# The second routing of an eight-block model: expert 0 computed for every token, seven experts routed

## The chip, the cores and the metric

The kernel runs on one core of one Trainium2 chip, as one launch written out engine by engine: five instruction streams (TensorE, VectorE, ScalarE, GpSimd and SyncE) that are ordered among themselves only by semaphores. The metric is the device time of the launch in microseconds, the median of the runs; lower is better.

## The reference, cut to what matters

Four layers, each an attention block and a feed-forward block, over x of 4 x 512 tokens of 128 values (float32). The change is in the feed-forward block of the third layer, a top-2 mixture of 8 experts with a capacity of 640 rows each (2 x 1.25 x 2048 / 8):

```python
logits = xf @ w_g                                   # xf: the 2048 normed tokens
topv, topi = jax.lax.top_k(logits, 2)
probs = softmax(logits where chosen, -1e9 elsewhere)
rank = cumulative count per expert, all first choices before all second choices
mask = one_hot(topi) * (rank < 640)
wts = sum(mask * probs)
cb[token, topi[:, k], rank_sel[k]] += wts[k]        # for k = 0, 1
exp_batches = einsum('nec,nd->ecd', cb != 0, xf)    # rows sent to the experts
h = gelu(einsum('ecd,edh->ech', exp_batches, c_fc), approximate=False)   # 128 -> 512
exp_out = einsum('ech,ehd->ecd', h, c_proj)                              # 512 -> 128
out = einsum('nec,ecd->nd', cb, exp_out)            # added to x by the caller
```

The next block is the cross attention of the fourth layer, and after it a mixture that computes 8 small experts for all tokens.

## The kernel before, in words

**Layout.** Tokens lie in 16 chunks of 128 (4 sequences t = 0 to 3, 4 chunks each). `xs` holds the normed tokens by rows, with the token's number as a 129th value, and `xT` holds them turned, 128 features by 512 tokens for each t. Eight PSUM banks `ps0` to `ps7` of 128 x 512 float32 serve everything.

**Order.** Each engine walks the same lists of stages, SEQ0 to SEQ3, with `wavefront`: stage s of sequence t runs beside stage s+1 of sequence t-1. Between SEQ2 and SEQ3 stands the second routing, named "m2" (the first, "m0", stands between SEQ0 and SEQ1 and has a capacity of 128 rows, so that nothing about it changes here). The order around the change is written out by hand, and a few semaphores carry it: `idx_ready` (row numbers known), `sent` (16 for each finished send), `g_ld`, `gT_m`, `gT_s` (an expert's rows fetched, turned, copied), `h_mm`, `h_act` (a hidden unit multiplied, activated), `gy_mm`, `gy_sb`, `gy_st` (an expert's result multiplied, copied out, stored).

**The second routing, stage by stage.**
- VectorE picks each token's first expert (L1464 to L1468). TensorE counts with matmuls over one-hot rows (L834, L837), VectorE makes row numbers (`places`, L1473 to L1480). GpSimd then sends, one indirect DMA for a chunk of 128 tokens and a choice (`send`, L1857): 16 for the first choices, 16 for the second. They write rows of 516 bytes to the table `tok2` in DRAM, 8 x 640 rows.
- Beside the first sends TensorE counts the second choices (`count_second`, L897 to L908) into bank 2, VectorE copies `first_n` out of it (L1713), makes the second row numbers, and computes the gate weights (L1715 to L1722). TensorE multiplies out keys and values of the next attention (`prepare("L3")`, L870 and L873), and VectorE copies them out (L1507, L1516).
- When all 32 sends have landed (`sent`), SyncE fetches the rows expert by expert (L543), and TensorE runs nine matmuls whose result is not used (`keep_busy`, L913) before it turns the first expert's rows (L949). GpSimd spreads the keys and values by heads (L1888, L1901).
- For each expert VectorE writes the turned rows as two parts, a rounded high part (L1588) and the remainder (L1589). The hidden layer is `product` (L915 to L919): three matmuls, high x high, high x low, low x high, on 320 tokens, for 4 slices f of 128 hidden units and 2 halves, so 24 matmuls. ScalarE applies Gelu from bank 2 + u % 4 into `hid` (L1229). The output layer is 20 float32 matmuls (L981, in the trace two entries for each, so 40). VectorE copies the result to `ysb` (L1614), and GpSimd stores it by five indirect DMAs to the table `res2` (L1930), 2 x 2048 rows, one half for each choice, which was set to zero at the start of the kernel.
- TensorE's order is hidden(0), then for each expert e: hidden(e+1), turning of group e+3, results(e). With five blocks an expert's result takes banks 6 and 7 both.
- After the last store SyncE reads `res2` back (L550), and VectorE adds both halves, weighted by `wgt`, to x (`fetched`, L1623), which is the first step of SEQ3.

**Memory that is shared.** `qTR` and `qT` lie in the same bytes (the attention's queries; `ysb` too lies there), as do `xTR` and `xT`, `bigR` and `big`. `kr` holds rounded keys of the earlier attentions; the one of the fourth layer uses `kvR`. The high parts of the first-layer weights of m2 lie in `ring_r`, the low parts in `moe_r`; both are made long before, beside the attention of SEQ2 (L1840, L1841).

## Time and profile before

| | us |
|---|---|
| median of 3 runs | 693.19 (693.09 to 694.12) |
| profiled execution | 696.29 |
| its span, first to last instruction | 694.5 |
| TensorE busy in the span | 507.6 (73%) |
| VectorE busy | 346.9 (50%) |
| GpSimd busy | 260.4 (37%) |
| ScalarE busy | 218.7 (31%) |
| mean granted TensorE clock | 0.796 of 2.4 GHz |

The profile is of one execution. Times in its rows are microseconds from the start of the span. "PEld" is TensorE's loading of weights, beside its matmuls. A matmul's duration contains the way through the array, and matmuls overlap: what one costs in a row of them is the distance from start to start. A group of matmuls in the timeline is given by its start, its length and its count. What ended an idle time is told from semaphore events; "remote" (in the chain: "another core or an unknown queue") stands where an event came with no instruction that ended just then. The chain follows the last instruction back to whatever released it.

### The profile page before, as it was taken

What the parts mean: (1) busy time and instruction counts of PE and PEld (TensorE: products, weight loads), DVE (VectorE), ACT (ScalarE), POOL (GpSimd) and SP (SyncE); (2) the same over time, 40 slices, a digit from 0 to 9 for tenths busy, and PEclk for the clock granted to TensorE, in tenths of its full rate; (3) what the DMA queues carried; (4) which work ended last, traced back from release to release, by engine and by line L of the source; (5) the groups of instructions that cost most, each with busy time, mean ns of one, the idle gap of its engine ahead of it and who ended that gap; (6) DMA issues with size and microseconds to landing.
All of it is one profiled execution on the core that took longest, in us unless ns stands there. A gap on an engine that the chain in (4) does not pass through costs nothing.

```text
span 694.5 us, 8672 instructions
## 1 busy us (share of the span) xinstructions
PE 507.6 (73%) x3053; PEld 382.2 (55%) x3053; DVE 346.9 (50%) x1111; ACT 218.7 (31%) x423; POOL 260.4 (37%) x372
## 2 busy tenths in 40 slices
PE   4497793648678865697863049998269957999997
PEld 3342472636555451443763029998035346899997
DVE  4749528641098643159874023331286684333333
ACT  3341542102234520051330005331044334344441
POOL 4650757371345101155337751555475051000000
PEclk9679797557865999589555569999659966899999
DMA  9998600001170006750001122111350000000002
GB/s 288 301 143 171 230 1 0 9 22 37 53 259 0 1 0 176 205 166 0 1 0 51 49 75 69 52 48 37 92 160 1 1 1 0 1 1 1 1 1 60
DMA packets 64107, 48.06 MB, mean 69 GB/s; under 512 B 6441, under 2 KB 55877, under 8 KB 63936
## 3 DMA queue, kind: packets, MB, share of 16 engines
q1 hardware_dynamic: 60560, 41.88, 23.3%
q0 software_dynamic: 3072, 5.06, 2.3%
q10 hardware_dynamic: 432, 0.57, 0.3%
q8 instruction: 24, 0.39, 0.2%
q14 instruction: 19, 0.16, 0.1%
HBM read 35.08 MB, written 13.68 MB: 70 GB/s over the span
## 4 chain that ended last, share of the span: by engine, by line
PE 52%; DVE 20%; POOL 10%; issue 7%; DMA 3%; ACT 3%; another core or an unknown queue 2%; SPq 1%; POOLq 0%; ACTq 0%; DVEq 0%
PE ps L1019 9%; PE ps L981 5%; POOL tok L1857 3%; PE ps L917 3%; DVE rz L1406 3%; PE ps L603 3%; DVE st L1319 3%; PE ps L919 3%; PE ps L918 3%; POOL rstd L1765 3%; PE ps L615 3%; PE ps L714 2%; PE ps L657 2%; PE ps L780 2%
## 5 line engine op out<-in xcount | busy, mean ns | idle before, releaser
L1930 POOL DMA_INDIRECT res<-qT,dest x48 | 47.1, 982 | 68.2 <-DVE qT L1614 57.7
L1640 DVE SCALAR_TENSOR_TENSOR x<-ps,gate,x 128x128 f32<-128x128 f32 x128 | 36.1, 345 | 62.9 <-PE ps L1019 62.9
L1019 PEld LDWEIGHTS ps<-moe_w,big 128*128 128x128 f32 x512 | 63.3, 196 | 3.9 <-issue 1.5
L1019 PE MATMUL ps<-moe_w,big 128*128 128x128 f32 x512 | 63.7, 280 | 0.0
L1244 ACT ACTIVATE big<-ps,col 128x512 f32<-128x512 f32 x64 | 44.0, 688 | 59.2 <-PE ps L919 58.8
L1774 POOL TENSOR_SCALAR negmean<-mv 128x4 f32<-128x4 f32 x44 | 11.3, 257 | 127.8 <-DVE mv L1322 126.7
L1857 POOL DMA_INDIRECT tok<-r,to_slot x48 | 47.3, 986 | 31.5 <-DVE to_slot L1480 17.8
L603 PE MATMUL ps<-con,xn 128*128 128x128 f32 x128 | 31.9, 398 | 35.3 <-DVE xn L1335 20.6
L913 PE MATMUL ps<-tri,ones 128*128 128x512 bf16 x46 | 17.7, 562 | 50.2 <-DMA tok<-r,to_slot 25.1
L1195 ACT ACTIVATE xn<-x,negmean,rstd 128x128 f32<-128x128 f32 x48 | 21.1, 486 | 98.8 <-POOL negmean L1777 98.8
L1229 ACT ACTIVATE big<-ps 128x320 f32<-128x320 f32 x64 | 26.7, 441 | 77.8 <-PE ps L919 77.6
L1765 POOL TENSOR_TENSOR rstd<-rstd,half 128x4 f32<-128x4 f32 (+1 forms) x45 | 47.8, 1062 | 3.7
L603 PEld LDWEIGHTS ps<-con,xn 128*128 128x128 f32 x128 | 21.4, 203 | 48.8 <-DVE xn L1335 48.5
L981 PE MATMUL ps<-moe_w,big 128*128 128x128 f32 x384 | 45.7, 275 | 2.7 <-DVE qT L1614 2.7
L981 PEld LDWEIGHTS ps<-moe_w,big 128*128 128x128 f32 x384 | 44.2, 192 | 3.0 <-issue 2.8
L1406 DVE RECIPROCAL rz<-ps 128x512 f32<-128x512 f32 x12 | 40.1, 3346 | 9.6 <-PE ps L733 9.4
L1614 DVE COPY qT<-ps 128x128 f32<-128x128 f32 (+1 forms) x24 | 9.4, 421 | 65.9 <-PE ps L981 40.7
L913 PEld LDWEIGHTS ps<-tri,ones 128*128 128x128 bf16 x46 | 5.7, 132 | 60.4 <-issue 33.6
L633 PE MATMUL ps<-sq,xT 128*128 128x128 f32 x128 | 20.6, 314 | 15.4 <-DVE xT L1408 15.4
L633 PEld LDWEIGHTS ps<-sq,xT 128*128 128x128 f32 x128 | 18.0, 219 | 23.7 <-DVE xT L1408 22.1
L1319 DVE BATCH_NORM_STATS2 st<-x 128x6 f32<-128x128 f32 x128 | 27.9, 281 | 5.8 <-DMA x<-in_x 4.8
L917 PE MATMUL ps<-qTR,moe_r 128*128 128x512 f32 x64 | 29.0, 453 | 2.0 <-DVE oh L1468 2.0
(283 smaller groups left out, 1153.4 us busy)
## 6 DMA issues: line engine op xcount, KB each, us to landing
ring<-in_ew SPq DMA_DIRECT2D x21, 256.0 KB, 5.3
moe_w<-in_m0w SPq DMA_DIRECT2D x16, 256.0 KB, 6.6
moe_w<-in_m2w SPq DMA_DIRECT2D x16, 256.0 KB, 5.8
big<-res SPq DMA_DIRECT2D x12, 256.0 KB, 4.6
moe_w<-in_ew SPq DMA_DIRECT2D x11, 256.0 KB, 5.5
tok<-zero SPq DMA_DIRECT2D x1, 2580.0 KB, 30.9
big<-tok SPq DMA_DIRECT2D x8, 322.5 KB
ring<-in_ewg SPq DMA_DIRECT2D x9, 256.0 KB, 4.6
```

What stands on the lines that cost most here:

```text
L603: last = nc.tensor.transpose(ps[2 * t][:, cols(c)], from_, ident)
L633: last = mm(ps[2 * t + 1][:, cols(c)], xT[0:width, t, cols(c)], w, start=True, stop=True)
L917: mm(o, high, x_high_, start=True, stop=False)
L981: last = mm(o, hid[:, e % 2, f, cols(b)], moe_w[:, e, 512 + P * f:512 + P * f + P], start=f == 0, stop=f == 3 and bias is None)
L1019: last = mm(ps[7 - i % 2][:, cols(c)], big[:, f, i % B, cols(c)], w[:, e, F + P * f:F + P * f + P], start=f == 0, stop=f == FC - 1)
L1244: A(big[:, f, i % B, :], ps[(i * FC + f) % 6][:, :], fn, bias=V(bias, e * FC + f)).then_inc(h_act, 1)
L1319: i = v.bn_stats(st[:, C * t + c, :], d[:, C * t + c, :])
L1406: link(v.reciprocal(rz[:, :], ps[2 * t + 1][:, :]))
L1640: last = v.scalar_tensor_tensor(out=x[:, C * t + c, :], in0=ps[7 - i % 2][:, cols(c)], scalar=gate[:, C * t + c, e:e + 1], in1=x[:, C * t ...
L1765: g_.tensor_tensor(rstd[0:rows, tt], rstd[0:rows, tt], half[0:rows, 0:width], ALU.pow).then_inc(done, 1)
L1857: g_.indirect_dma_start(out=tok_d[name], out_offset=bass.IndirectOffsetOnAxis(ap=to_slot[:, j:j + 1], axis=0), in_=xs[:, j % (B * C), :], ...
L1930: g_.indirect_dma_start(out=res_d[name], out_offset=bass.IndirectOffsetOnAxis(ap=dest[:, at:at + 1], axis=0), in_=ysb[:, e % 2, cols(b)], ...
```

## The change

Expert 0 is no longer routed. It is computed for all 2048 tokens from `xT`, four units of 512 tokens, and the outcome is added to x with the weight `have`, each token's gate for expert 0 in either choice (0 where it was not chosen or over the capacity). Experts 1 to 7 go the old way. All 32 sends stay, the rows for expert 0 too, but these are no longer fetched. The changed parts:

```diff
+        units0 = {"m0": 0, "whole": 4 * E, "m2": 4 * E + C * B}
+        done0 = {"m0": 0, "whole": E, "m2": E + B}
-        PLACED = {"m0": dict(cap=CAP0, eg=4, ranks=1), "m2": dict(cap=CAP2, eg=1, ranks=2)}
+        PLACED = {"m0": dict(cap=CAP0, eg=4, ranks=1, whole=0), "m2": dict(cap=CAP2, eg=1, ranks=2, whole=1)}
+            a["n"] = E - a["whole"]
+        whole_low = kr[:, :].rearrange("p (a n) -> p a n", a=2)
+        whole_y = xn
 # TensorE, in placed("m2"): after count_second and the wait for the second row numbers, ahead of prepare("L3")
+            def whole_expert(loaded):
+                pe.wait_ge(loaded, 32 * E)
+                pe.wait_ge(split, 8)
+                def hidden(t):
+                    pe.wait_ge(low_ready, t + 1)
+                    for f in range(4):
+                        if t >= 1:
+                            pe.wait_ge(h_act, n["h"] - 3)
+                        product(ps[2 + f][:, :], w1_high["m2"][:, 0, cols(f)], w1_low["m2"][:, 0, cols(f)],
+                                qTR[:, t, :], whole_low[:, t % 2, :])
+                        n["h"] += 1
+                    return n["h"]
+                def results(t, units):
+                    pe.wait_ge(h_act, units)
+                    if t >= 2:
+                        pe.wait_ge(gy_sb, done0["whole"] + t - 1)
+                    for c in range(C):
+                        for f in range(4):
+                            last = mm(ps[6 + t % 2][:, cols(c)], hid[:, t % 2, f, cols(c)], moe_w[:, 0, 512 + P * f:512 + P * f + P],
+                                      start=f == 0, stop=f == 3)
+                    last.then_inc(gy_mm, 1)
+                units = hidden(0)
+                for t in range(B):
+                    nxt = hidden(t + 1) if t + 1 < B else None
+                    results(t, units)
+                    units = nxt
 # ScalarE: whole_high() after SEQ2, whole_expert(Gelu) after the exponentials of the gates
+            def whole_high():
+                for t in range(B):
+                    act.wait_ge(xT_ready, 4 * WHOLE_TURN + t + 1)
+                    A(qTR[:, t, :], xT[:, t, :], ACT.Identity).then_inc(x_high, 1)
+            def whole_expert(fn):
+                for t in range(B):
+                    if t >= 2:
+                        act.wait_ge(gy_mm, done0["whole"] + t - 1)
+                    for f in range(4):
+                        act.wait_ge(h_mm, n["h"] + 1)
+                        A(hid[:, t % 2, f, 0:S], ps[2 + f][:, :], fn).then_inc(h_act, 1)
+                        n["h"] += 1
 # VectorE
+            def whole_low_of(t):
+                dve.wait_ge(x_high, t + 1)
+                if t >= 2:
+                    dve.wait_ge(h_mm, units0["whole"] + C * (t - 1))
+                v.tensor_tensor(whole_low[:, t % 2, :], xT[:, t, :], qTR[:, t, :].bitcast(F32), ALU.subtract).then_inc(low_ready, 1)
+            def whole_out(t):
+                dve.wait_ge(gy_mm, done0["whole"] + t + 1)
+                v.tensor_copy(whole_y[:, chunks(t), :], ps[6 + t % 2][:, :].rearrange("p (c d) -> p c d", c=C)).then_inc(gy_sb, 1)
             places(ps[2][:, E:(nb + 1) * E]..., slice(nb, 2 * nb), CAP2, "base2")
+            whole_low_of(0)
+            whole_low_of(1)
...
             link(v.tensor_reduce(wgt[:, :], gb[:, :, :], AX.X, ALU.add))
+            link(v.tensor_tensor(have[:, 0:nb], gb[:, 0:nb, 0], gb[:, nb:2 * nb, 0], ALU.add))
+            whole_low_of(2)
+            whole_out(0)
+            whole_low_of(3)
+            for t in range(1, B):
+                whole_out(t)
             prepared("L3")
 # VectorE, in evacuate, for each of the seven experts, ahead of the wait for its result
+                    if name == "m2":
+                        for c in range(nb * i_ // a["n"], nb * (i_ + 1) // a["n"]):
+                            i = v.scalar_tensor_tensor(out=x[:, c, :], in0=whole_y[:, c, :], scalar=have[:, c:c + 1], in1=x[:, c, :],
+                                                       op0=ALU.mult, op1=ALU.add)
+                        link(i)
```

Elsewhere the loops over the experts of a routing run over `a["n"]` (8 for m0, 7 for m2), with e = i + `a["whole"]`, and the counts that are waited for begin at `units0` and `done0`. GpSimd issues 35 stores where there were 40, SyncE seven fetches where there were eight.

## Rows read from the trace of the kernel before

**Rows 1.** The page: shares of the chain that ended last, by engine.

```profile
PE 52%; DVE 20%; POOL 10%; issue 7%; DMA 3%; ACT 3%; another core or an unknown queue 2%; SPq 1%; POOLq 0%; ACTq 0%; DVEq 0%
```

**Rows 2.** The chain of 355 to 520 us: start, length, engine and line.

```profile
404.15 2.04 DMA tok<-r,to_slot
...
406.50 4.00 PE ps L913 x9
...
423.56 4.47 PE ps L981 x40
...
494.87 2.08 DMA res<-qT,dest
```

**Rows 3.** Busy time of each engine in stretches; PEclk is the granted clock.

```profile
core 0: us, PE busy (x) PEld busy (x) DVE busy (x) ACT busy (x) POOL busy (x), PEclk, DMA share, GB/s
...
378.80:406.20 27.40, 2.50 (x10) 2.21 (x10) 3.10 (x10) 0.00 (x0) 20.23 (x21) 0.50 0.15 50
406.50:412.20 5.70, 5.06 (x14) 2.22 (x14) 0.60 (x1) 0.00 (x0) 5.05 (x5) 0.50 0.42 116
412.30:482.00 69.70, 64.70 (x507) 63.29 (x507) 22.60 (x61) 28.35 (x65) 29.18 (x30) 1.00 0.19 54
...
428.02:436.98 8.96, 8.96 (x74) 8.96 (x73) 2.98 (x8) 3.44 (x8) 4.89 (x5) 1.00 0.21 58
```

**Rows 4.** Timeline of VectorE: the copying out of experts 0, 1 and 6.

```profile
428.06 0.89 DVE L1614 COPY qT<-ps 128x512 f32<-128x512 f32 x2 [6.89 <-PE ps L981]
...
437.04 0.89 DVE L1614 COPY qT<-ps 128x512 f32<-128x512 f32 x2 [5.89 <-PE ps L981]
...
481.25 0.89 DVE L1614 COPY qT<-ps 128x512 f32<-128x512 f32 x2 [7.87 <-remote]
```

**Rows 5.** Timeline of TensorE in the last mixture, whose hidden product has 512 columns.

```profile
603.78 1.95 PE L1019 MATMUL ps<-moe_w,big 128*128 128x128 f32 x16
...
606.04 0.39 PE L919 MATMUL ps<-qTR,moe_r 128*128 128x512 f32 x1
606.27 0.39 PE L917 MATMUL ps<-qTR,moe_r 128*128 128x512 f32 x1
...
606.97 1.28 PE L1019 MATMUL ps<-moe_w,big 128*128 128x128 f32 x10
```

**Rows 6.** Groups by shape, 592 to 694 us and 406 to 497 us: count, busy, mean ns.

```profile
L1244 ACT ACTIVATE big<-ps,col 128x512 f32<-128x512 f32 x56 | 38.5, 688 | 58.4 <-PE ps L919 58.2
...
L1589 DVE TENSOR_TENSOR xTR<-ps,bigR 128x512 fp32r<-128x512 f32 x8 | 5.5, 692 | 0.3
```

**Rows 7.** Timeline at the end of the counting and at `prepare("L3")`.

```profile
369.57 1.03 PE L906 MATMUL ps<-oh,ones 128*128 128x120 bf16 x15
...
377.39 0.17 DVE L1713 COPY first_n<-ps 128x8 f32<-128x8 f32 x1 [7.63 <-remote]
...
378.63 0.20 DVE L1480 TENSOR_SCALAR to_slot<-slot 128x16 uint32<-128x16 f32 x1
...
379.47 1.92 PE L873 MATMUL ps<-sq,rep 128*128 128x128 f32 x8
...
381.10 0.35 DVE L1507 TENSOR_SCALAR kts<-ps,col 128x128 f32<-128x128 f32 x1
...
392.03 0.69 DVE L1516 TENSOR_TENSOR vr<-ps,row 128x512 f32<-128x512 f32 x1 [10.58 <-remote]
```

**Rows 8.** Timeline of the first routing: VectorE's adds beside GpSimd's sends.

```profile
137.93 4.30 DVE L1651 SCALAR_TENSOR_TENSOR x<-r,drop,x 128x128 f32<-128x128 f32 x16
138.75 0.97 POOL L1857 DMA_INDIRECT tok<-r,to_slot  x1 [0.30 <-issue]
140.03 0.97 POOL L1857 DMA_INDIRECT tok<-r,to_slot  x1 [0.30 <-issue]
```

**Rows 9.** Timeline from the last send to the first expert's transposes and product.

```profile
410.29 1.27 PE L949 MATMUL ps<-con,big 128*128 128x128 f32 x5
...
414.52 0.39 PE L917 MATMUL ps<-bigR,ring_r 128*128 128x320 f32 x1
```

More of the change, by code:

```diff
@@ L105 @@
 BUSY = 14
+WHOLE_TURN = sum(q[0] == "turn" for q in SEQ0 + SEQ1 + SEQ2) - 1
 LAST_TURN = sum(q[0] == "turn" for q in SEQ0 + SEQ1 + SEQ2 + SEQ3) - 1
@@ L541, in placed_traffic @@
                         sp.wait_ge(gT_s, g0 + g - 1)
-                    rows = slice(g * a["gb"] * P, (g + 1) * a["gb"] * P)
+                    rows = slice((a["whole"] + g) * a["gb"] * P, (a["whole"] + g + 1) * a["gb"] * P)
                     sp.dma_start(xg[:, g % 2, 0:a["gb"] * (D + 1)].rearrange("p (b d) -> p b d", d=D + 1),
@@ L951, in turn_group, with hidden @@
                     n["g"] += 1
-                def hidden(e):
-                    g = e // eg
+                def hidden(i):
+                    g, e = i // eg, i + a["whole"]
                     pe.wait_ge(gT_s, g0 + g + 1)
-                    at = (e % eg) * a["cap"]
+                    at = (i % eg) * a["cap"]
                     for f in range(4):
@@ L989, in placed @@
                 units = hidden(0)
-                for e in range(E):
-                    nxt = hidden(e + 1) if e + 1 < E else None
-                    results(e, units)
+                for i in range(a["n"]):
+                    nxt = hidden(i + 1) if i + 1 < a["n"] else None
+                    results(i, units)
                     units = nxt
@@ L1216, in chances @@
                 n["moe"] += 1
+            def whole_high():
[10 more added lines that the diff above has]
+                        n["h"] += 1
             def placed(name, k, fn, bias):
                 a = PLACED[name]
-                for e in range(E):
-                    if e >= 2:
-                        act.wait_ge(gy_mm, k * E + e - 1)
-                    if name == "m2" and e == 1:
+                for i in range(a["n"]):
+                    e = i + a["whole"]
+                    if i >= 2 or name == "m2":
+                        act.wait_ge(gy_mm, done0[name] + i - 1)
+                    if name == "m2" and i == 1:
                         round_keys("L3")
@@ L1593, in group @@
                     number = xg[:, g % 2, 0:gb_ * (D + 1)].rearrange("p (b d) -> p b d", d=D + 1)[:, :, D]
-                    at = (40 if k else 0) + g * gb_
+                    at = (40 if k else 0) + (a["whole"] + g) * gb_
                     if a["ranks"] == 1:
@@ L1604, in evacuate @@
                 group(1)
-                for e in range(E):
-                    g = e // eg
-                    if e % eg == eg - 1 and g + 2 < a["groups"]:
+                for i_ in range(a["n"]):
+                    g = i_ // eg
+                    if i_ % eg == eg - 1 and g + 2 < a["groups"]:
                         group(g + 2)
-                    dve.wait_ge(gy_mm, k * E + e + 1)
-                    if e >= 2 or k:
-                        dve.wait_ge(gy_st[e % 2], stores(name, e // 2))
+                    if name == "m2":
+                        for c in range(nb * i_ // a["n"], nb * (i_ + 1) // a["n"]):
+                            i = v.scalar_tensor_tensor(out=x[:, c, :], in0=whole_y[:, c, :], scalar=have[:, c:c + 1], in1=x[:, c, :],
+                                                       op0=ALU.mult, op1=ALU.add)
+                        link(i)
+                    dve.wait_ge(gy_mm, done0[name] + i_ + 1)
+                    if i_ >= 2 or k:
+                        dve.wait_ge(gy_st[i_ % 2], stores(name, i_ // 2))
                     for j in range(0, nb_, 4):
                         m = min(4, nb_ - j)
-                        i = v.tensor_copy(ysb[:, e % 2, j * P:(j + m) * P], ps[6 + (j // 4 if nb_ > 4 else e % 2)][:, 0:m * P])
+                        i = v.tensor_copy(ysb[:, i_ % 2, j * P:(j + m) * P], ps[6 + (j // 4 if nb_ > 4 else i_ % 2)][:, 0:m * P])
                     i.then_inc(gy_sb, 1)
@@ L1925, in deliver @@
                 a = PLACED[name]
-                for e in range(E):
-                    pool.wait_ge(gy_sb, seen * E + e + 1)
+                for i in range(a["n"]):
+                    pool.wait_ge(gy_sb, done0[name] + i + 1)
                     for b in range(a["nb"]):
-                        at = (40 if seen else 0) + e * a["nb"] + b
+                        at = (40 if seen else 0) + (i + a["whole"]) * a["nb"] + b
                         g_.indirect_dma_start(out=res_d[name], out_offset=bass.IndirectOffsetOnAxis(ap=dest[:, at:at + 1], axis=0),
-                                              in_=ysb[:, e % 2, cols(b)], in_offset=None, bounds_check=a["ranks"] * B * S - 1,
-                                              oob_is_err=False).then_inc(gy_st[e % 2], 16)
+                                              in_=ysb[:, i % 2, cols(b)], in_offset=None, bounds_check=a["ranks"] * B * S - 1,
+                                              oob_is_err=False).then_inc(gy_st[i % 2], 16)
             g_.memset(zero[:, 0:D], 0.0)
```

29 lines of the change are left out of this document (16 added, 13 removed).

## The prediction

> **What bounds the kernel now.** I read the shares of the chain first, then the chain in the second routing, then busy time by stretch, then the timelines. TensorE has 52% of the chain [rows 1]: work that leaves TensorE's path counts, where nothing else is late in its place. In the second routing the chain goes three ways [rows 2]. Up to 404.15 us it is GpSimd's sends, one after another, the last one landed at 406.19. From 406.50 it is TensorE (warm-up matmuls, then the experts). The end is the last store, 494.87 + 2.08. The stretches say why the two halves differ [rows 3]: from 378.80 to 406.20 TensorE is busy for 2.50 of 27.40 us and ScalarE for none, while from 412.30 to 482.00 TensorE has 64.70 of 69.70. The reader is to see an idle engine ahead of a full one. The experts follow each other in TensorE's own time: the copies of experts 0 and 6 start at 428.06 and 481.25 [rows 4], six periods in 53.19, so 8.87 us each. Inside one (428.02 to 436.98) TensorE is busy throughout, VectorE 2.98 us, ScalarE 3.44, GpSimd 4.89 [rows 3]. So one routed expert less is worth 8.87 us, if what replaces it fits ahead of the sends' end.
>
> **What the change removes.** One period of 8.87 us on the path: 24 hidden matmuls, 5 transposes, 40 output entries, 8 activations, VectorE's splitting and copying, five stores, one fetch. The first and the last period keep their neighbours (the last two experts, where GpSimd's stores are the chain, are still 6 and 7), so an inner period goes. The 32 sends stay, and so does their end at 406.19.
>
> **What it adds on TensorE.** For each of four t: 12 products on 512 columns and 16 float32 matmuls, 32 entries. The last mixture shows both forms at full clock [rows 5]: products start 0.23 us apart, and a period from 603.78 to 606.97, 3.19 us, holds 16 output entries and 6 products. With 4.47 us for 40 output entries [rows 2], 0.112 each, 16 take 1.79, and the 6 products the other 1.40, 0.233 each. The whole expert is 48 x 0.233 = 11.2 and 128 x 0.112 = 14.3, together 25.5 us.
>
> **When it can start.** It stands behind the wait for the second row numbers, written at 378.63 + 0.20 = 378.83 [rows 7], and needs the first low part. That subtraction with two SBUF inputs is not in the trace on VectorE; the nearest are the same subtraction with one input in PSUM, 0.69 us [rows 6], and the adds with two SBUF inputs, 4.30 / 16 = 0.27 for 128 columns [rows 8], 1.08 for 512. I take 0.69, since it is the same operation and width: start 379.5. (1.08 would cost 0.4 once.) `qTR` is written by ScalarE before, four copies into an engine that has nothing to do between the last turn and the gates' exponentials; nothing if hidden, 4 x 0.69 = 2.8 if not, still ahead of 378.8.
>
> **The clock.** Up to 406.20 the granted clock is 0.50, 1.2 GHz [rows 3]: TensorE did almost nothing. At the warm-up matmuls it stays at 0.50 for 5.70 us of nearly full work and is 1.00 behind it. I expect the same 5.7 us at the start of the whole expert, which does half the work in it: 2.85 lost. Bounds: 0 and, if the clock never rose, 25.5 more.
>
> **The other engines beside it.** ScalarE: 16 activations of 128x512 by 0.688 [rows 6], 11.0 us of 25.5. Hidden unit t+1 needs bank f back from unit t, four groups of products (2.8 us at full clock) later, so ScalarE's 0.69 for each is in time. VectorE: four low parts and four copies, 8 x 0.69 = 5.5 us; the gate weights wait 1.4 us longer, which nobody does. `have` is one small instruction, 0.3. The 16 adds to x are 4.3 us [rows 8], two or three in each of seven periods, 0.5 to 0.8 on a VectorE that has 2.98 of 8.96: nothing; without that cover 4.3.
>
> **What is late next.** Whole expert: 379.5 + 25.5 + 2.85 = 407.9, so 1.7 behind the sends' landing. `prepare("L3")` now stands behind it: VectorE copies out t = 3 (0.69), then the keys (0.35) and the values (0.69) [rows 6, 7], until 409.7. Queued behind that wait on TensorE are the nine warm-up matmuls; they took 4.00 us [rows 2] at half the clock and should take half of it now: 411.7. Before, the first transposes began at 410.29 [rows 9], so they are 1.4 late; at full clock five take about 0.3 less. Net 1.1 late. GpSimd's spreading of the keys starts about 1.7 later; its user is ScalarE's rounding at 418.8 in the chain, with 7 us to spare.
>
> **The sum.** In the profiled execution: -8.87 + 1.1 = -7.8, 696.29 to 688.5. Not all of it need be paid in other runs. VectorE's copy of `first_n` waits until 377.39, though TensorE's last counting matmul ends at 370.60 [rows 7]. If that signal came in time, the row numbers would be there at 372.0, the whole expert would end at 401.1, and the transposes would wait for nothing new: -8.9, and up to -9.9 if the clock is still up for the warm-up matmuls. The profiled execution is 3.1 us above the median of the runs, so some such wait may be absent from these. I take -8.2, between the two: 693.19 - 8.2 = 685.0 us.
>
> **Rivals.** *Late signals of TensorE during the sends (the other side).* The trace shows two signals of TensorE that arrive long after its matmul ended, both while GpSimd sends: 370.60 to 377.39, 6.8 us, and the values of `prepare` (381.39) to 392.03, 10.6 us [rows 7]. Before, sends hid both. The whole expert has 20 such signals, and ScalarE, then TensorE, wait for them. TensorE can run on for 2.8 us, the next unit's products. One of 10.6 costs 7.8 and eats the gain: 693.2. Two, 10.6 and 6.8, cost 7.8 + 4.0: -7.8 + 11.8, 697.2. It decides from 7.8 us of lost TensorE time on. For it: two long ones among a few in this very stretch. Against it: between 412.30 and 482.00, with stores 29 of 70 us, TensorE is busy for 64.70 and its signals hold up no expert but the last ones [rows 3, 4]. One or two of some 3 to 5 us (part of the gain lost) is more likely: -4, 689.2.
>
> The Trainium skill, SBUF — State Buffer, "Who interferes with whom", says that TensorE and ScalarE never wait on anyone for SBUF, since they have their own ports. By that rule alone TensorE would signal in time and the sum would be -8.9, 684.3; the trace has the two, whatever their cause, so I keep this rival's chances above what the rule would leave.
>
> *The sends are slowed by VectorE.* Eight new instructions of 128x512 run beside sends. If each held GpSimd up for its length, the sends would end 8 x 0.69 = 5.5 later, at 411.7, behind the whole expert: -8.9 + 5.5 = -3.4, 689.8. Against it: in the first routing 16 adds with two SBUF inputs ran from 137.93 for 4.30 us, and sends still started 1.28 apart [rows 8], as in the chain.
>
> *It does not do what it says:* a clock that stays at 0.50 through all of the whole expert. 2 x 25.5 = 51 us from 379.5 end at 430.5, 24.3 behind the sends: -8.9 + 24.3 + 1.7 for `prepare` = +17, 710. Against it: the clock rose at every long run of products seen here [rows 3].
>
> **How the numbers follow.** About 0.2% (1.4 us) is what a measurement of this kernel tells from no change. The forecast (-7 to -10) has 0.58, part of the gain lost 0.17, slower sends 0.04, late signals from 7.8 us on 0.18 (half of it near no change or slightly either way), cold clock 0.03. Faster by over 0.2%: 0.58 + 0.17 + 0.04 = 0.79, less 0.02 for part losses that come near zero, 0.77. Within 0.2%: 0.08. Slower: 0.15. The forecast's own range is 683.3 to 686.5. The range for 8 in 10 goes from 683.0 (-10.2: the better end and a clock that is up) to 693.0, which takes in part losses and slower sends.
>
> **What would show it.** In the profile after: between 379 and 408 TensorE over 90% busy, with PEclk 1.00 from about 385; products on `qTR` and `whole_low` of line `product`; the last copy of `whole_y` near 408 (or 401); the last send unchanged, some 41 us after the first; the warm-up matmuls 0.21 us apart and not 0.43; seven copies of `ysb` 8.87 apart; the last store at 489 instead of 497. Wrong would be: TensorE idle in gaps of several us in the whole expert with ScalarE or VectorE waiting for it (late signals), sends further apart than 1.28, or periods above 8.9 us, which would mean that VectorE's adds are no longer hidden.

## The result, and the profile after

The changed kernel takes 706.82 us (median of 4 runs, 702.80 to 707.63), the kernel before beside it on the same chip 693.14 (691.04 to 694.12): a ratio of 1.0191, 95% interval [1.0152, 1.0229]. It is slower by 13.7 us, where 8.2 us faster was predicted. The time is outside the range of 683 to 693.

The profiled execution of after took 702.8 us, its span 701.0. Everything in it up to the second routing came early: its first send starts at 358.22, that of before at 364.45. In the profiles of this case, of kernels that are alike almost up to that moment, it lies between 357.7 and 364.5, so absolute times of two profiles can't be set against each other. I therefore measure two stretches, each from one event to another of the same profile. **A** is from GpSimd's first send of the second routing to ScalarE's first hidden unit of a routed expert. **B** is from there to the first tile of rows fetched back.

The timeline of VectorE and GpSimd after, at these events and between (start, length, engine, line, what, idle before):

```profile
358.22 1.13 POOL L1938 DMA_INDIRECT tok<-r,to_slot  x1 [8.53 <-DVE to_slot L1538]
...
398.44 0.97 POOL L1938 DMA_INDIRECT tok<-r,to_slot  x1 [0.30 <-issue]
```

```profile
403.98 0.69 DVE L1639 COPY xn<-ps 128x512 f32<-128x512 f32 x1 [20.81 <-PE ps L948]
...
422.36 0.69 DVE L1639 COPY xn<-ps 128x512 f32<-128x512 f32 x1 [2.88 <-PE ps L948]
...
443.46 0.89 DVE L1687 COPY qT<-ps 128x512 f32<-128x512 f32 x2 [5.89 <-issue]
...
487.99 0.89 DVE L1687 COPY qT<-ps 128x512 f32<-128x512 f32 x2 [7.42 <-issue]
...
508.28 2.31 DVE L1696 SCALAR_TENSOR_TENSOR x<-big,wgt,x 128x128 f32<-128x128 f32 x8 [11.34 <-DMA big<-res]
```

The sends are nearly as before, 32 of them, 1.27 us apart but for two, the last one started 40.2 us after the first (before 39.7). The experts are as predicted too: from the first to the sixth copy of results 44.53 us, 8.91 a period (before 8.87, [rows 4]). What is wrong is the whole expert. Its first group of results leaves PSUM at 403.98 and its last at 422.36, where the prediction had the last at 28.4 us behind its first product. ScalarE's timeline shows what happened beside the sends: each row of L1270 is one hidden unit, released by the third product of its group.

```profile
373.56 0.60 ACT L1270 ACTIVATE big<-ps 128x512 f32<-128x512 f32 x1 [10.34 <-PE ps L925]
374.83 0.60 ACT L1270 ACTIVATE big<-ps 128x512 f32<-128x512 f32 x1 [0.68 <-issue]
377.46 0.60 ACT L1270 ACTIVATE big<-ps 128x512 f32<-128x512 f32 x1 [2.03 <-PE ps L925]
382.38 0.60 ACT L1270 ACTIVATE big<-ps 128x512 f32<-128x512 f32 x1 [4.32 <-remote]
386.58 0.60 ACT L1270 ACTIVATE big<-ps 128x512 f32<-128x512 f32 x1 [3.60 <-issue]
390.77 0.60 ACT L1270 ACTIVATE big<-ps 128x512 f32<-128x512 f32 x1 [3.60 <-remote]
397.07 0.60 ACT L1270 ACTIVATE big<-ps 128x512 f32<-128x512 f32 x1 [5.70 <-remote]
403.38 0.60 ACT L1270 ACTIVATE big<-ps 128x512 f32<-128x512 f32 x1 [5.70 <-remote]
...
413.17 2.64 ACT L1270 ACTIVATE big<-ps 128x512 f32<-128x512 f32 x4 [3.73 <-PE ps L925]
```

The eight units that need no result came 29.82 us from the first to the eighth, 4.3 us each on the average. The first two were on time, at the ends of their third products (373.52 and 374.80); the last six gaps are between 2.6 and 6.3, so the lateness grew from unit to unit. Behind the sends, four take 2.64 us. TensorE's own timeline shows that its products were long issued:

```profile
379.23 0.40 PE L925 MATMUL ps<-qTR,moe_r 128*128 128x512 f32 x1
383.03 0.50 PE L923 MATMUL ps<-qTR,ring_r 128*128 128x512 f32 x1 [3.40 <-issue]
...
383.83 4.40 PE L948 MATMUL ps<-moe_w,big 128*128 128x128 f32 x23
389.37 0.27 PE L948 MATMUL ps<-moe_w,big 128*128 128x128 f32 x1 [1.14 <-issue]
...
392.17 0.37 PE L948 MATMUL ps<-moe_w,big 128*128 128x128 f32 x1 [1.73 <-issue]
...
403.39 0.55 PE L948 MATMUL ps<-moe_w,big 128*128 128x128 f32 x1 [1.06 <-issue]
403.60 0.78 PE L923 MATMUL ps<-qTR,ring_r 128*128 128x512 f32 x1
```

By these rows the 24th product was through at about 384, yet ScalarE got its unit at 403.38, 19 us later. From 389 on TensorE starts one entry in 1.75 us (eight gaps in 14.02) and its idle time is given as "issue": no semaphore that the profile shows released it. (The gap ahead of 383.03 is another kind: that product waited for the bank of ScalarE's fourth unit, which ended at 382.98.) The reader is to see that the engine's records tell when a matmul was started, and that its users were released much later. I read this as ends that come through slowly and make room for the next entries slowly; the profile shows the starts and the releases, not the ends themselves. The stretches show it once more (columns as in [rows 3]): from 358 to 399 TensorE has matmuls on record for 18.74 of 41.00 us, and the mean granted clock is 0.62, so it is at 1.2 GHz most of the time, where the plan had 2.4 from about 385 on.

```profile
core 0: us, PE busy (x) PEld busy (x) DVE busy (x) ACT busy (x) POOL busy (x), PEclk, DMA share, GB/s
358.00:399.00 41.00, 18.74 (x101) 15.65 (x102) 10.20 (x42) 5.77 (x9) 31.33 (x32) 0.62 0.15 49
...
404.00:423.00 19.00, 19.00 (x128) 17.38 (x128) 3.29 (x6) 4.79 (x8) 0.00 (x0) 0.89 0.03 9
```

After the sends TensorE is full (19.00 of 19.00): three quarters of the whole expert's results and half of its products are paid in full behind the sends. A grew from 50.8 us (364.45 to 415.25) to 72.4 (358.22 to 430.65), B shrank from 85.5 to 77.6. The sum, +21.6 - 7.9 = +13.7, is the difference of the medians. (The two profiled executions are only 6.5 us apart, because the first send of after came 6.2 us sooner.)

### The profile page after: what moved, and what is told of

Read it like the earlier page. It is cut to its first block and busy times, and to the rows that moved or that the text cites. A ratio compares the mean times of both kernels' runs of the same rounds, so it can differ in the third digit from the quotient of the medians.

```text
span 701.0 us, 8911 instructions
## 1 busy us (share of the span) xinstructions
PE 527.4 (75%) x3160; PEld 400.0 (57%) x3160; DVE 353.5 (50%) x1128; ACT 226.1 (32%) x435; POOL 255.7 (36%) x367
## 5 line engine op out<-in xcount | busy, mean ns | idle before, releaser
L1059 PEld LDWEIGHTS ps<-moe_w,big 128*128 128x128 f32 x512 | 63.2, 196 | 4.2 <-issue 1.8
L2011 POOL DMA_INDIRECT res<-qT,dest x43 | 41.8, 972 | 61.8 <-DVE qT L1687 52.7
L1059 PE MATMUL ps<-moe_w,big 128*128 128x128 f32 x512 | 63.6, 280 | 0.3 <-DVE x L1704 0.3
L1464 DVE RECIPROCAL rz<-ps 128x512 f32<-128x512 f32 x12 | 40.2, 3346 | 9.6 <-PE ps L739 9.4
L1021 PE MATMUL ps<-moe_w,big 128*128 128x128 f32 x344 | 42.7, 282 | 2.8 <-DVE qT L1687 2.8
L1021 PEld LDWEIGHTS ps<-moe_w,big 128*128 128x128 f32 x344 | 41.3, 198 | 3.1 <-issue 3.0
L919 PE MATMUL ps<-tri,ones 128*128 128x512 bf16 x46 | 18.1, 574 | 25.2 <-DMA big<-res 19.4
L1285 ACT ACTIVATE big<-ps 128x320 f32<-128x320 f32 x56 | 23.2, 441 | 41.5 <-PE ps L925 41.3
L925 PE MATMUL ps<-qTR,moe_r 128*128 128x512 f32 x80 | 33.8, 422 | 0.0
L923 PE MATMUL ps<-qTR,moe_r 128*128 128x512 f32 x64 | 28.8, 449 | 2.0 <-DVE oh L1526 2.0
```

The source lines that it names most:

```text
L923: mm(o, high, x_high_, start=True, stop=False)
L925: mm(o, low, x_high_, start=False, stop=True).then_inc(h_mm, 1)
L1021: last = mm(o, hid[:, i % 2, f, cols(b)], moe_w[:, e, 512 + P * f:512 + P * f + P], start=f == 0, stop=f == 3 and bias is None)
L1059: last = mm(ps[7 - i % 2][:, cols(c)], big[:, f, i % B, cols(c)], w[:, e, F + P * f:F + P * f + P], start=f == 0, stop=f == FC - 1)
L1464: link(v.reciprocal(rz[:, :], ps[2 * t + 1][:, :]))
L2011: g_.indirect_dma_start(out=res_d[name], out_offset=bass.IndirectOffsetOnAxis(ap=dest[:, at:at + 1], axis=0), in_=ysb[:, i % 2, cols(b)], ...
```

## The experiments

Theory A throughout: GpSimd's row-addressed sends hold the ends of TensorE's matmuls back. The rivals are the whole expert's own cost, the queue and the bytes of the sends, and a fixed delay of a signal. One table first, since each verdict rests on it. First send (that of the second routing; in e3 it is SyncE's), A and B are of one profile each.

| | first send | A | B | run, us (n) |
|---|---|---|---|---|
| before | 364.45 | 50.8 | 85.5 | 693.14 (4), later 695.95 (7), 695.80 (19), 696.71 (22) |
| after | 358.22 | 72.4 | 77.6 | 706.82 (4) |
| e1, no whole expert | 359.72 | 52.0 | 78.1 | 684.47 (4) |
| e2, whole expert after the sends | 357.68 | 79.2 | 79.4 | 713.49 (4) |
| e3, plain sends by SyncE | 360.75 | 45.7 | 78.5 | 680.32 (1) |
| e5, plain sends by GpSimd | 357.80 | 45.0 | 79.6 | 677.91 (1) |
| e4, one product per unit | 362.02 | 67.3 | 79.7 | 704.16 (1) |
| e6, 16 sends | 360.22 | 53.4 | 79.7 | 687.46 (1) |
| e7, sends that write nothing | 363.28 | 70.5 | 78.9 | 706.05 (1) |
| v1, whole expert late | 364.26 | 52.9 | 83.9 | 694.33 (10) |
| v2, one group beside | 363.56 | 56.7 | 84.7 | 699.75 (10) |
| v3, v1 mended | 360.94 | 52.9 | 77.3 | 692.86 (12) |
| v4, v2 mended | 364.31 | 56.8 | 77.5 | 696.37 (10) |

Before moved by up to 3.6 us from one session to the next, after was measured in the first alone, and five of the runs are single ones. For these five the stretches A and B bear the verdict, not the time. The 695.95 stands beside e1, e2, e3 and e5, the 695.80 beside e4, e6, v1 and v2, the 696.71 beside e7, v3 and v4.

**e1_seven_no_whole.** In `placed` of TensorE:

```diff
-                if name == "m2":
-                    whole_expert(loaded)
```

and with it `whole_high`, ScalarE's part, the low parts, `whole_out` and the adds to `x`.

> Expert 0 is left out of the second routing altogether: no whole expert, no adds to x, seven routed experts. Both theories of the loss (TensorE held back by the sends; the whole expert slow by itself) agree here: one period of 8.9 us goes and nothing comes, so 693.1 - 8.9 = 684.2 us. If it came out above 686, a routed expert would be worth less than its period, and part of the loss would lie behind the whole expert, not in it.

684.47 us (683.71 to 686.97), before on the same chip 695.95, ratio 0.9868 [0.9799, 0.9938]. The routed experts are worth what was predicted: seven copies, the first six 8.87 us apart (424.04 to 468.40 in five periods), and the time is 0.3 us from the 684.2 expected. By the ratio that is 9.2 us less than before, by its interval 4 to 14, so the period and not the time fixes the price. The loss is in the whole expert, all of it: 22 us between this kernel and after.

**e2_whole_after_sends.** One wait ahead of the whole expert:

```diff
                 if name == "m2":
+                    pe.wait_ge(sent, 16 * 3 * B * C)
                     whole_expert(loaded)
```

> As the changed kernel, but TensorE waits for the landing of all 32 sends before the whole expert. Theory A (the sends hold TensorE's completions back): the whole expert takes its own 25.5 us plus 2.9 for the clock, some 28.4 us from 406.2 on, with units of three products 1.28 us apart at half clock and 0.70 at full; ScalarE never waits over 1 us for one of them; the time is 693.1 - 8.9 + 28.4 + 1 = 713.6, only 7 us worse than the changed kernel although nothing overlaps. Theory B (the whole expert is slow by itself: its operands, its banks, its handshake with ScalarE): it takes some 40 us again, as it did beside the sends (372 to 422 there, 50 us), and the time is 725 or more.

713.49 us (711.74 to 717.23), ratio 1.0300 [1.0225, 1.0374], and the same units of ScalarE, now with no send beside them:

```profile
401.92 0.60 ACT L1271 ACTIVATE big<-ps 128x512 f32<-128x512 f32 x1 [39.24 <-PE ps L925]
403.19 0.60 ACT L1271 ACTIVATE big<-ps 128x512 f32<-128x512 f32 x1 [0.68 <-PE ps L925]
404.30 4.11 ACT L1271 ACTIVATE big<-ps 128x512 f32<-128x512 f32 x6 [0.51 <-PE ps L925]
```

```profile
400.26 0.77 PE L923 MATMUL ps<-qTR,ring_r 128*128 128x512 f32 x1 [36.45 <-DMA tok<-r,to_slot]
...
427.50 0.39 PE L876 MATMUL ps<-col,sq 128*128 128x128 f32 x2
```

From its first product to the next piece of work the whole expert takes 27.24 us here, against 50.26 in after (371.90 to 422.16). So its operands, its banks and its waits for ScalarE are not at fault: 23.0 us are added beside the sends. After and e2 differ by only 6.7 us in the medians (7.6 by the ratios): 41 us of sends hid a quarter of a 27 us expert.

**e3_sends_by_SyncE** and **e5_plain_sends_by_GpSimd.** Both replace the 32 row-addressed sends by plain ones of the same 128 rows to consecutive places, so the experts get other rows; e3 issues them on SyncE's queue, e5 on GpSimd's. e5's edit:

```diff
             def send(name, j):
+                if name == "m2":
+                    g_.dma_start(out=tok_d[name][j * P:(j + 1) * P, :], in_=xs[:, j % (B * C), :]).then_inc(sent, 16)
+                    return
```

> As the changed kernel, but the 32 writes of 128 rows to the table are plain DMAs issued by SyncE, to rows 128 j and not by index (so the experts get other rows than the reference's). Theory A1 (GpSimd's software-made sends hold TensorE back): with these gone the whole expert runs at its own pace, units 1.28 then 0.70 us apart, done 26 to 29 us after its start. Theory A2 (any write from SBUF to DRAM of this size does): units are late by 2 us and more as long as these writes run. Theory B: 40 us or more, whatever sends the rows. The time itself says little, since the writes end far earlier; under A1 the table is ready in under 20 us, and the whole expert, not the sends, sets the start of the routed experts.

> As the changed kernel, but GpSimd issues the 32 writes as plain DMAs (rows 128 j) and not by index. If making descriptors on GpSimd or its queue is what holds TensorE back, the whole expert is as slow as in the changed kernel (units 4 to 6 us apart), 700 to 707 us. If it is the index (128 descriptors of one row, small writes all over the table), units come at 1.28 and 0.70 us and the time is some 685 or less.

680.32 and 677.91 us. In e3 ScalarE's eight units are through 7.5 us after the first (371.36 to 378.90), beside SyncE's sends (360.75 to 376.98), and the whole expert takes 28.3 us. e5's rows, GpSimd's sends and ScalarE's units beside them:

```profile
357.80 17.13 POOL L1939 DMA_DIRECT2D tok<-r  x32 [8.25 <-DVE to_slot L1538]
```

```profile
367.86 0.60 ACT L1270 ACTIVATE big<-ps 128x512 f32<-128x512 f32 x1 [5.10 <-PE ps L925]
369.14 0.60 ACT L1270 ACTIVATE big<-ps 128x512 f32<-128x512 f32 x1 [0.68 <-PE ps L925]
370.41 4.07 ACT L1270 ACTIVATE big<-ps 128x512 f32<-128x512 f32 x6 [0.67 <-PE ps L925]
378.21 2.62 ACT L1270 ACTIVATE big<-ps 128x512 f32<-128x512 f32 x4 [3.73 <-PE ps L925]
```

A plain send costs GpSimd 0.54 us (17.13 / 32) instead of 1.27, and TensorE's ends come on time: the eight units are through at 374.48, the sends at 374.93. The queue views say that it is the same queue with the same packets, and nearly the same bytes (first after, then e5, both from 355 to 402 us):

```profile
q0 software_dynamic: 1024, 2.03, 13.1%
```

```profile
q0 software_dynamic: 1024, 2.12, 13.7%
```

So this queue, this number of packets and these bytes do not hold TensorE back by themselves. What differs is that the sends are addressed row by row. (These sends also end some 24 us sooner, so of the whole expert only what runs beside them, 366 to 375 us, bears on it: 24 products, where in after the third unit was already late 4 us behind the first product.)

A second signal in every profile says the same. TensorE's last counting matmul is started beside the first sends, and VectorE, idle since, copies `first_n` when its end is reported. That idle time is 5.16 to 8.45 us in all eleven profiles with row-addressed sends (7.63 in before, 6.22 in after, 5.16 in e7), and 0.97 and 0.98 in e3 and e5, the two with plain ones. GpSimd being busy does not seem to be enough either: in before it multiplied from 406.44 to 411.55, and the last of 14 matmuls started from 406.50 on, over at 411.56, released VectorE at 411.60.

**e4_one_product_per_unit.** In `hidden` of the whole expert, the low parts are left out of the sums:

```diff
-                        product(ps[2 + f][:, :], w1_high["m2"][:, 0, cols(f)], w1_low["m2"][:, 0, cols(f)],
-                                qTR[:, t, :], whole_low[:, t % 2, :])
+                        mm(ps[2 + f][:, :], w1_high["m2"][:, 0, cols(f)], qTR[:, t, :], start=True, stop=True).then_inc(h_mm, 1)
```

> The changed kernel, but each hidden unit of the whole expert is one product (high part by high part) instead of three; the low parts are left out of its sums, so its output is less precise. Everything else, the 32 sends by GpSimd included, stays. Theory A (while GpSimd's row-addressed sends are on their way, each instruction of TensorE reports its end some 1.4 to 2.1 us after the one before it, so the delay goes by the number of instructions): ScalarE's Gelu units beside the sends come 1.4 to 2.1 us apart instead of the 4 to 6 us of the changed kernel; all eight that need no result are through by about 389 us of the span, the results of group 0 (16 instructions) follow beside the sends, and the last one of the whole expert is out at about 408 to 412 us instead of 422; the run takes 692 to 697 us. Theory B (a fixed delay of the signal between engines, whatever the number of instructions): the units stay 4 to 6 us apart and the run takes 703 to 706 us, shorter only by the products' own 0.2 us each.

704.16 us. The eight units came from 378.69 to 387.10, 1.20 us each for one product, beside 1.42 for each of three in after (29.82 / 21): not the 4 to 6 of theory B. The average hides two paces: five units were on time, 0.5 us each, and the last three came 1.4, 2.9 and 2.1 us behind the one before. The total was not as theory A said: A is 67.3, 5.1 less than after's, and the run is 7 us over the upper end of 692 to 697, within theory B's 703 to 706. The first group's 16 float32 matmuls of results were held instead:

```profile
378.69 2.56 ACT L1269 ACTIVATE big<-ps 128x512 f32<-128x512 f32 x5 [11.67 <-issue]
...
387.10 0.60 ACT L1269 ACTIVATE big<-ps 128x512 f32<-128x512 f32 x1 [1.52 <-remote]
407.70 2.07 ACT L1269 ACTIVATE big<-ps 128x512 f32<-128x512 f32 x4 [20.01 <-remote]
```

My figure for the rest was wrong: I had the first group's results follow beside the sends and the whole expert's last ones out at 408 to 412. VectorE copied the first group's at 407.61, nearly 6 us after the last send had started (401.86), the second's at 412.06 and the last at 420.15. The delay grows with the instructions that are waiting, but not at one rate: none for the first few, 1.2 to 1.4 us for a product on the average, and TensorE started one instruction in 2.45 us at the end (391.30 to 406.00, six gaps). So a fixed delay is out by the units' spacing, and not by the time of the run.

**e6_first_choices_only.** The 16 sends of the second choices are left out.

```diff
-            for j in range(B * C, 2 * B * C):
-                send("m2", j)
-            pool.wait_ge(sent, 16 * 3 * B * C)
+            pool.wait_ge(sent, 16 * 2 * B * C)
```

> The changed kernel, but only the 16 sends of the first choices are issued; the 16 of the second choices are left out, so half of the routed rows hold nothing new. Everything else stays. Theory A (the row-addressed sends hold TensorE's ends back only as long as they run): the slow stretch ends with the last send, about 20 us after the first, at 378 to 380 us of the span; from there ScalarE's units come 1.28 us apart or less, and the whole expert is through at about 400 to 404 us instead of 422: the run takes 684 to 690 us. Theory B (the whole expert is slow for a reason of its own: its waits, its clock at 1.2 GHz, its operands): the units stay 4 to 6 us apart up to about 398 us, the end of the whole expert comes before 418 us by no more than the clock explains, and the run takes 700 us or more.

687.46 us, as theory A said (684 to 690). The 16 sends start from 360.22 to 379.65, and SyncE's first fetch, which waits for the landing, at 381.95. The whole expert started at 376.10, so that little of it ran beside them; its third unit came 3.2 us late, and from there on the units run:

```profile
377.75 0.60 ACT L1270 ACTIVATE big<-ps 128x512 f32<-128x512 f32 x1 [12.50 <-issue]
379.03 0.60 ACT L1270 ACTIVATE big<-ps 128x512 f32<-128x512 f32 x1 [0.68 <-issue]
383.10 3.05 ACT L1270 ACTIVATE big<-ps 128x512 f32<-128x512 f32 x6 [3.47 <-PE ps L925]
389.77 2.64 ACT L1270 ACTIVATE big<-ps 128x512 f32<-128x512 f32 x4 [3.63 <-PE ps L925]
```

The same instructions with the same operands are slow beside sends and quick once these have stopped: the whole expert takes 29.0 us, and A is 19.0 us less than in after, for sends that start over 19.4 us instead of 40.2.

**e7_sends_to_nowhere.** All 32 sends, whose bound drops nearly every row:

```diff
-                                      in_=xs[:, j % (B * C), :], in_offset=None, bounds_check=E * PLACED[name]["cap"] - 1,
+                                      in_=xs[:, j % (B * C), :], in_offset=None, bounds_check=(0 if name == "m2" else PLACED[name]["cap"] * E - 1),
```

> The changed kernel, with all 32 row-addressed sends of the second routing issued as before, but with a bound that drops all rows but those for slot 0: the routed rows stay unwritten, and so most rows of results aren't stored either. Theory A1 (it is GpSimd's own work for a row-addressed send, the reading of 128 row numbers, that holds TensorE's ends back): the units of ScalarE stay 4 to 6 us apart beside the sends, and the preparation of the keys starts about 64 us after the first send, as in the changed kernel. Theory A2 (it is the scattered writes on the way to memory): the units come 1.28 us apart or less beside the sends, and the preparation starts at most 45 us after the first send.

706.05 us. The queue moved 0.02 MB instead of 2.03, and the ends were late all the same:

```profile
q0 software_dynamic: 992, 0.02, 1.5%
```

```profile
389.08 0.60 ACT L1270 ACTIVATE big<-ps 128x512 f32<-128x512 f32 x1 [2.24 <-remote]
392.61 0.60 ACT L1270 ACTIVATE big<-ps 128x512 f32<-128x512 f32 x1 [2.93 <-remote]
398.24 0.60 ACT L1270 ACTIVATE big<-ps 128x512 f32<-128x512 f32 x1 [5.03 <-remote]
409.10 1.09 ACT L1270 ACTIVATE big<-ps 128x512 f32<-128x512 f32 x2 [10.26 <-remote]
```

The preparation of the keys starts 61.9 us after the first send (425.2), in after 63.9, and the first group's results are out 33.3 us after the first product (375.69 to 408.99), in after 32.1. The eight units came sooner than the 4 to 6 us apart of theory A1, 3.0 on the average (377.34 to 398.24), so the bytes may have a part in their pace, but the stretch as a whole kept its length. So it isn't the traffic. GpSimd's own work for a row-addressed transfer is what is left of the causes that I tried; no run isolates it. The Trainium skill, *DMA: Bandwidth & Descriptors*, "SWDGE vs HWDGE vs iDMA", says that a DMA issued from GpSimd has its descriptors computed by software on GpSimd's cores, the plain ones as well as the indirect ones. No run here shows that work by itself; e7 fits it (the cost stays when the bytes go), but by the page e5's transfers are built there too, and they do no harm.

**v1_none_beside** and **v2_one_group_beside** move the whole expert. TensorE is idle for 14.0 us behind the last routed expert (e1), so v1 puts all four groups there and v2 three, with VectorE adding them from PSUM to `x`. In both, the first routing's result rows lie over weights of the slot experts, so their output is another one; the instructions are the same. v1 has 4 warm-up matmuls ahead of the next attention and v2 has 14 (3.19 us); they start behind the first fetched tile, outside A and B. The core of the edit, at the end of TensorE's `placed`:

```diff
+                if name == "m2":
+                    for k_, t in enumerate(LATE):
+                        nxt = whole_hidden(LATE[k_ + 1], False) if k_ + 1 < len(LATE) else None
+                        whole_results(ps[6 + k_ % 2], late_hid[:, 1 - k_ % 2, :, :], units, done0["late"] + (k_ - 1 if k_ >= 2 else 0))
+                        units = nxt
```

> A version of the changed kernel with the full output: of the whole expert's four groups of 512 tokens only the first is computed beside the sends; the other three follow the last routed expert, where TensorE otherwise stood idle for 14.0 us (seven routed experts without a whole one), and their results are added from PSUM straight to x. Theory A: the one group costs nothing beside the sends (28 instructions there instead of up to 112), the preparation of the keys starts at about 400 us of the span. The three late groups have 19 us of TensorE's own time at full clock against 14 us of idle, and run beside GpSimd's last row-addressed stores: 5 to 9 us are added to the 684.5 us without the whole expert: 689 to 694 us. Theory B (a delay that does not go by the instructions beside the sends): the preparation still starts at 404 us or later, 694 to 699 us.

> As the version with one group beside the sends, with all four groups after the last routed expert, so TensorE has nothing beside the sends but the folding of the queries and a short stretch of matmuls for its clock. Theory A: no delay beside the sends; four late groups of 6.4 us each, 25.5 us, against 14 us of idle: 11 to 15 us are added to 684.5 us: 695 to 700 us, about 6 us above the version with one group beside. Theory B (the delay is that of the whole expert's own instructions wherever they stand): the four groups take as long late as they took beside the sends, some 50 us, and the run takes over 715 us.

v2 takes 699.75 us, ratio 1.0069 [1.0038, 1.0100], over both of its ranges, and v1 694.33 (693.80 without its slowest run), ratio 0.9961 [0.9923, 1.0000], just under its 695 to 700. The order is the other way round than I had expected. One group beside the sends is not free, as I had it in theory A for v2: A is 56.7 with it and 52.9 without, 3.8 us for 7 us of work. And B is no shorter for one late group less (84.7, 83.9), because VectorE waited for the first two late groups before it took up any of the four fetched tiles:

```profile
490.72 1.13 DVE L1649 SCALAR_TENSOR_TENSOR x<-ps,have,x 128x128 f32<-128x128 f32 x4 [9.35 <-remote]
499.29 1.13 DVE L1649 SCALAR_TENSOR_TENSOR x<-ps,have,x 128x128 f32<-128x128 f32 x4 [7.45 <-PE ps L946]
...
501.06 2.31 DVE L1706 SCALAR_TENSOR_TENSOR x<-big,wgt,x 128x128 f32<-128x128 f32 x8
```

**v3_whole_after_experts** and **v4_one_group_beside** mend that (in v4 no late group is added ahead of the tiles), and give the two routings separate result rows (v3 keeps the 4 warm-up matmuls, v4 the 14). v3 against v1:

```diff
-                if name == "m2" and t in LATE[2:]:
+                if name == "m2" and t in LATE[1:]:
...
-            for k_ in range(2):
-                whole_late(k_)
-            dve.wait_ge(gy_sb, done0["late"] + 2)
+            whole_late(0)
+            dve.wait_ge(gy_sb, done0["late"] + 1)
```

> The version with none of the whole expert beside the sends, with two changes: the first routing's result rows stand apart from the second's, so that its output is the reference's, and VectorE adds the late group t only when it has come to tile t of the fetched rows, instead of holding all four tiles back for the first two groups. Theory A (what is left of the price is the order on VectorE): the first tile starts at about 492 us of the span instead of 501, the four tiles with 5.2 us each are through at about 515 us instead of 519.1; 3 to 5 us below the 694.3 us of the version it is made from: 689 to 692 us, ratio to before 0.990 to 0.995. Theory B (TensorE's late results set the end): results for the last group are out no sooner than 504 us and the last tile ends as before: 693 to 696 us.

> As the version with the whole expert after the routed experts, but the first group of 512 tokens is computed beside the sends and added there; three groups are late. Theory A: beside the sends the 28 instructions of one group still end late (in the earlier version of this kind the preparation of the keys came about 4 us later than without it), and one late group less gives back at most what it takes, so 688 to 695 us. Theory B (one group beside the sends is free): 684 to 688 us.

v3 takes 692.86 us (12 runs, 688.43 to 695.06), before beside it 696.71 (22 runs): ratio 0.9949 [0.9925, 0.9974]. It beats both kernels, before by 3.6 us by the ratio and after, by the two ratios, by about 17. v4 takes 696.37, ratio 0.9990 [0.9962, 1.0017], no different from before, and over its 688 to 695: the one group beside the sends costs what v3 gains (A 56.8 against 52.9). v3's first tile starts at 491.08, as theory A said (492):

```profile
488.20 1.13 DVE L1650 SCALAR_TENSOR_TENSOR x<-ps,have,x 128x128 f32<-128x128 f32 x4 [9.36 <-remote]
...
491.08 2.31 DVE L1707 SCALAR_TENSOR_TENSOR x<-big,wgt,x 128x128 f32<-128x128 f32 x8 [1.04 <-DMA big<-res]
...
513.04 0.68 DVE L1430 TENSOR_REDUCE mx<-ps 128x16 f32<-128x512 f32 x1
```

Its account: A +2.1, B -8.2, and from the first tile to the first attention maxima 21.96 us against 19.48 before (500.74 to 520.22), +2.5 for the late adds. That is -3.6 us, the measured gain. The median is 0.9 us over the 689 to 692 expected, in a session in which before too was 3.6 us slower than in the first; the ratio is within 0.990 to 0.995.

## Why the prediction was wrong

The price of a period was right: 8.87 us expected, 8.87 in e1 and 8.91 in after. VectorE's adds are hidden. The whole expert's own time was right: 25.5 + 2.85 = 28.35 against 27.24 without sends beside it (e2) and 27.34 in e5. The low part took 0.65 to 0.69 us (0.69 taken). The sends were hardly slowed: one of them, at 371.15 beside the first low parts (371.07), took 1.45 us instead of 0.97, and all 32 took 0.5 us more than before, where that rival needed 5.5. So is the cold clock out as a cause: it rose with the first products (0.95 from 377 to 384 us) and fell back to 0.50 (392 to 404) when TensorE stood still between entries, and it rose again in the 19 us after 404. The late signal of the last counting matmul was there again (6.22 us of waiting before `first_n` at 369.74), so the whole expert started 13.7 us after the first send, 1.4 sooner than in the prediction.

**The step that failed** is "what is late next": that the whole expert fits in the 27 us beside the sends and ends 1.7 us behind them. It ended at 422.16, some 22 us behind the landing of the last send (started at 398.44; the fetch that waits for it at 400.67). This is the rival of late signals, to which I gave 0.18. Its mechanism was right and its size was not. I priced it as one or two signals late by 10.6 and 6.8 us, each hiding 2.8 us: 693 to 697 us. The runs show no single late signals but a slow stretch. While row-addressed sends run, TensorE's work comes through at a low rate and the lateness adds up: none for the first two units, 1.2 to 1.4 us for a product on the average, more later. 40 instructions (24 products, 16 matmuls of results) needed the 32 us from 371.90 to 403.98, and half the products and three quarters of the results were still to come. The two late signals of [rows 7] I now take for the same thing, seen behind 32 short counting matmuls (6.8 us) and ten of `prepare` (10.6). With it the allowance was wrong that each late signal hides 2.8 us.

The evidence I used against it was read wrongly. I took 412.30 to 482.00 of before, with stores for 29 of 70 us, as a stretch where TensorE isn't held [rows 3]. These stores are row-addressed too, but TensorE's periods there stay 8.87 us, and I made of that a rule for the sends. The tail of v3 shows that stores can hold it: with the late groups beside the last stores four units came at

```profile
480.17 0.60 ACT L1279 ACTIVATE big<-ps 128x512 f32<-128x512 f32 x1 [6.07 <-PE ps L929]
482.28 0.60 ACT L1279 ACTIVATE big<-ps 128x512 f32<-128x512 f32 x1 [1.51 <-remote]
483.69 1.32 ACT L1279 ACTIVATE big<-ps 128x512 f32<-128x512 f32 x2 [0.82 <-remote]
```

and the first late group's results, whose hidden units ended at 474.10, were out at 488.20, when the last store, started at 485.08, was gone. Why five stores in a period of 8.87 us cost the routed experts nothing, while 32 sends end to end cost 23 us, is open. A difference that the trace shows: in a period the five are followed by a gap of 2.85 us, and v3's late units fall beside ten stores without one (473.59 to 485.08). No run varies the gap.

By the rule of the Trainium skill, *SBUF — State Buffer*, "Who interferes with whom" (TensorE and ScalarE never wait on anyone for SBUF), the time would have been 684.3. That section is about SBUF and silent on the way by which a matmul reports its end; the measurement decides. I had kept the rival above what the rule leaves it, but not far enough: [rows 7] had two late signals in that very stretch.

**What stays open.** The runs show that the row-addressed transfers of GpSimd do it, and not their queue, the number of their packets or their bytes, and that it is over within 4 us of their landing. They don't show what GpSimd and TensorE share. That plain GpSimd transfers don't do it rests on one profile, e5: 9 us of the whole expert, and the one signal of the counting. I tried no row-addressed sends with pauses between them.

## What to carry to other kernels

An idle engine is free room only if its results reach their users in that stretch: before moving work there, look in the trace for how long its few instructions' ends took to arrive, and read late ones as the pace of that stretch, not as accidents. Beside a long run of GpSimd's row-addressed transfers, TensorE's work was almost as dear as behind them (706.8 against 713.5 us). Put such work elsewhere, as v3 does behind the routed experts, and let each consumer wait for its own group alone.

## What the runs showed of the hardware that I had not expected

- Beside 32 row-addressed sends (1.27 us each, 41 us) a chain of products and results ran at 50.3 us instead of 27.2; with the sends' bytes taken away (2.03 MB to 0.02) the delay stayed, with plain sends on the same queue (1024 packets each) it went.
- VectorE waited 5.2 to 8.5 us for the end of the counting in all eleven profiles with row-addressed sends, and under 1 us in the two with plain ones.
- A plain transfer of 128 rows cost GpSimd 0.54 us, a row-addressed one 1.27: e5 and e3 have A 5.8 and 5.1 us under before's even with the whole expert in it.
- A record of TensorE in this stretch does not tell when its users are released: the row at 379.23 looks finished at 379.63, and its unit, the seventh, reached ScalarE at 397.07. "issue" as the cause of idle time on TensorE, and "remote" on ScalarE, often went with it.
- The first send moved by up to 6.8 us between profiles of kernels that are almost alike up to it (357.68 to 364.45), so that stretches had to be measured inside one profile.
